# Moving VectorE's checks, maxima chain and statistics behind its own products, and two blocks of most chunks from VectorE to GpSimd, in a three-layer graph attention kernel

## The reference

```python
def gat_layer(x, src, dst, W, a_src, a_dst, b, n_nodes):
    h = x @ W
    s = h @ a_src
    d = h @ a_dst
    e = leaky_relu(s[src] + d[dst], 0.2)
    m = segment_max(e, dst)
    ex = exp(e - m[dst])
    z = segment_sum(ex, dst)
    alpha = ex / z[dst]
    return segment_sum(alpha[:, None] * h[src], dst) + b

h = relu(layernorm(x))
h = relu(gat_layer(h, ..., W1, a_src1, a_dst1, b1))      # layer 0: 128 -> 256
x = x + gat_layer(h, ..., W2, a_src2, a_dst2, b2)        # layer 1: 256 -> 128
h = relu(layernorm(x))
x = x + gat_layer(h, ..., W, att_src, att_dst, bias)     # layer 2: 128 -> 128, 1e-16 added to z
```

## Time and profile before

| | us |
|---|---|
| median of 3 runs | 685.88 (685.61 to 686.31) |
| the profiled execution's own time | 684.96 |
| its span (first to last record) | 683.1 |
| counting stage with chunk 0, until chunk 1's blocks | 205 |
| chunk 1, chunk 2 | 33.1, 36.4 |
| chunks 3, 4 and 5 | 38.3, 35.0, 36.1 |
| chunks 6, 7, 8 and 9 | 36.7, 32.3, 32.4, 34.7 |
| chunks 10 to 13 | 36.6, 29.7, 29.2, 29.2 |
| chunk 14 to the start of its last products, and the rest | 30.3, 8.1 |
| busy: PE, DVE | 591.5 (87%), 639.8 (94%) |
| busy: ACT, POOL | 484.3 (71%), 460.1 (67%) |

### The profile page before, as it was taken

How to read it: one execution, slowest core, us unless ns; L and a number is a source line. 1 busy time by engine, 2 the same in 40 slices (tenths; PEclk the granted TensorE clock), 3 DMA queues, 4 the chain that set the end, 5 groups by cost and what they waited for, 6 DMA issues and landing times.

```text
span 683.1 us, 13824 instructions
## 1 busy us (share of the span) xinstructions
PE 591.5 (87%) x5571; PEld 573.1 (84%) x5571; DVE 639.8 (94%) x911; ACT 484.3 (71%) x719; POOL 460.1 (67%) x448
## 2 busy tenths in 40 slices
PE   1729865899978999999999899999989989999994
PEld 1628755789878999899989799999988979999994
DVE  3999999999999989999987998999998899999993
ACT  0416544656969688887666788989886698888891
POOL 5579101889928565775954675858598678697883
PEclk9978986899999999999999999999999999999999
DMA  2410002000000000000100100000010010110001
GB/s 70 119 56 2 1 7 6 35 2 1 20 1 1 20 1 20 2 1 8 26 14 1 27 1 20 2 19 1 8 20 20 1 27 6 35 32 8 20 1 42
DMA packets 22325, 12.07 MB, mean 18 GB/s; under 512 B 12393, under 2 KB 20055, under 8 KB 22255
## 3 DMA queue, kind: packets, MB, share of 16 engines
q1 hardware_dynamic: 21455, 9.85, 6.3%
q0 software_dynamic: 800, 1.26, 0.6%
HBM read 9.47 MB, written 1.64 MB: 16 GB/s over the span
## 4 chain that ended last, share of the span: by engine, by line
DVE 51%; PE 29%; issue 8%; DMA 5%; POOL 4%; ACT 2%; POOLq 0%; DVEq 0%
PE ps L1813 21%; DVE scratch L951 20%; DVE ps L1067 15%; DVE scratch L1149 5%; DMA xr<-in_x 3%; POOL scratch L751 2%; DVE ps L1069 2%; DVE ps L1079 1%; PE ps L1866 1%; PE ps L1821 1%; PE ps L1844 1%; DVE scratch L1067 1%; DMA gathered<-in_edges,start_i 1%; DVE gathered L1149 1%; PE ps L1780 1%
## 5 line engine op out<-in xcount | busy, mean ns | idle before, releaser
L1813 PE MATMUL ps<-hB,scratch 125*125 125x129 f32 x3450 | 404.5, 276 | 21.1 <-DVE scratch L1149 17.6
L1813 PEld LDWEIGHTS ps<-hB,scratch 125*125 125x125 f32 x3450 | 390.9, 189 | 28.4 <-DVE scratch L1149 22.6
L751 POOL TENSOR_TENSOR scratch<-scratch,C 125x625 f32<-125x625 f32 x239 | 304.3, 1285 | 113.0 <-ACT scratch L1569 110.9
L1067 DVE SCALAR_TENSOR_TENSOR ps<-C,a_unit,ps 125x625 f32<-125x625 fp8e3 x330 | 275.4, 866 | 2.3
L1567 ACT ACTIVATE scratch<-gathered,r_neg 125x625 f32<-125x625 f32 x219 | 176.6, 806 | 20.3 <-PE ps L1813 19.2
L1569 ACT ACTIVATE scratch<-scratch,r_src 125x625 f32<-125x625 f32 x219 | 178.9, 817 | 7.1
L1452 ACT ACTIVATE C<-ps 125x1000 fp8e3<-125x1000 f32 x80 | 78.2, 1001 | 77.9 <-PE ps L1780 77.7
L1780 PE MATMUL ps<-scratch 128*128 128x125 bf16 x1250 | 93.4, 239 | 32.7 <-DVE scratch L951 30.7
L1780 PEld LDWEIGHTS ps<-scratch 128*128 128x128 bf16 x1250 | 85.7, 108 | 39.9 <-DVE scratch L951 37.8
L1149 DVE SCALAR_TENSOR_TENSOR scratch<-ps,r_src,C 125x625 f32<-125x625 f32 x121 | 104.1, 860 | 5.4 <-PE ps L1803 5.3
L951 DVE TENSOR_TENSOR scratch<-key_lo,ps 128x4096 bf16<-128x4096 bf16 (+3 forms) x41 | 89.3, 2178 | 0.0
(11 more groups left out here) (195 smaller groups left out, 444.6 us busy)
## 6 DMA issues: line engine op xcount, KB each, us to landing
gathered<-g_lines SPq DMA_DIRECT2D x15, 305.2 KB
xr<-in_x SPq DMA_DIRECT2D x1, 1562.5 KB
out<-xr SPq DMA_DIRECT2D x4, 312.5 KB
edge_sb<-in_edges SPq DMA_DIRECT2D x1, 805.7 KB
gathered<-ext_lines SPq DMA_DIRECT2D x5, 122.1 KB
w<-in_W SPq DMA_DIRECT2D x2, 128.0 KB
out<-xr SPq DMA_DIRECT2D x1, 187.5 KB
out<-xr SPq DMA_DIRECT2D x1, 125.0 KB
```

The costliest lines, as they stand in the source:

```text
L751: g.tensor_tensor(slot[s], slot[s], C5[:, q % NC, s, :], ALU.mult).then_inc(pool_done, 1)
L1067: v.scalar_tensor_tensor(dest, counts, unit[:, s:s + 1], top, ALU.min, ALU.max).then_inc(S.top_done, 1)
L1813: last = mm(ps[0:P, acc_at(t):acc_at(t) + HW], A[:, P * t:P * (t + 1)], feat, start=opens and t in (0, 3), stop=closes, skip_group_check=True)
```

## The change

It does three things.

**Later places.** MODE_AT puts the checks of chunks 6 and 11 at block 17 in place of block 2. In the tables for chunks 6 to 9 the chain goes from (2, 2, 3, 3) to (4, 4, 4, 5), kappa from 4 to 5, the sums' inverse from block 4 to 6, the statistics from 9 to 10. In chunk 1 the transposes go from block 14 to 16, and all that stands behind them by one or two blocks.

**Two blocks by POOL alone.** The table ALONE names blocks by layer: in layer 0 (chunks 2 to 4) 7, 9, 18 and 19, of which those are taken that ACT and POOL don't have already, which is two for each chunk (7 and 18 in chunks 2 and 4, 9 and 19 in chunk 3); in layers 1 and 2 blocks 8 and 20, for all chunks but the turns. These 22 blocks had been DVE's own products. POOL now makes each with a tensor_scalar and a product.

**What follows from it.** by_pool counts them among POOL's; first_maximum picks the buffer of row factors and the source factors by chunk and layer, and waits for the load at a chunk's first such block; ACT's loop leaves them out.

```diff
+        MODE_AT = 17
...
         FIRST_LAYER = (None,
-                       At(14, (15, 15, 16, 16), 16, (17, 17, 18), None, (23,), (21, 23, 27), (23, 25, 29), 25, 27),
+                       At(16, (17, 17, 18, 18), 18, (19, 19, 20), None, (24,), (23, 25, 29), (25, 27, 31), 27, 29),
...
         USUAL = (At(1, (3, 4, 5, 6), 6, (8, 9, 10), None, (14,), (12, 15, 21), (14, 17, 23), 18, 20),
-                 At(1, (2, 2, 3, 3), 4, (4, 4, 4), (9, 9), (11, 15), (15, None, 17), (14, 16, 19), None, None),
+                 At(1, (4, 4, 4, 5), 5, (6, 6, 6), (10, 10), (11, 15), (15, None, 17), (14, 16, 19), None, None),
...
         BEFORE_LAST = (At(1, (3, 4, 5, 6), 6, (8, 9, 10), None, (14,), (12, 14, 19), (13, 16, 21), 17, 18),
-                       At(1, (2, 2, 3, 3), 4, (4, 4, 4), (9, 9), (11, 15), (15, None, 17), (14, 16, 19), None, None))
+                       At(1, (4, 4, 4, 5), 5, (6, 6, 6), (10, 10), (11, 15), (15, None, 17), (14, 16, 19), None, None))
...
-        POOL_OF = tuple(pool_tiles(q) for q in range(Q))
+        ALONE = ((7, 9, 18, 19), (8, 20), (8, 20))
+
+        def alone(q):
+            return tuple(s for s in ALONE[q // NC] if s not in pool_tiles(q)) if q > 1 and not turn(q) else ()
+
+        POOL_OF = tuple(tuple(sorted(pool_tiles(q) + alone(q))) for q in range(Q))
...
         def by_pool(q, s):
-            return q == 0 and not (s % 4 == 3 and s < 16) or q == 1 and s < SECOND
+            return q == 0 and not (s % 4 == 3 and s < 16) or q == 1 and s < SECOND or s in alone(q)
...
-                if s == 0:
+                if s == min(p for p in POOL_OF[q] if by_pool(q, p)):
                     pool.wait_ge(ga_loaded, 16 * (q + 1))
...
-                g.tensor_scalar(slot[s], ga[q], LARGEST, r_src[0][:, s:s + 1], ALU.min, ALU.max).then_inc(first_max, 1)
+                g.tensor_scalar(slot[s], ga[q % 2], LARGEST, r_src[q // NC % 2][:, s:s + 1], ALU.min, ALU.max).then_inc(first_max, 1)
...
-                    if L and c == 1 and s == 2:
+                    if L and c == 1 and s == MODE_AT:
                         over_nodes(2 * L, ext_all, all_ready)
                         set_mode(L)
```

2 lines of the change are left out of this document (1 added, 1 removed).

## The result

The change makes the kernel slower: 694.59 us (693.76 to 695.49) against 685.75 us for the kernel before, a ratio of 1.0133 with a 95% interval of 1.0121 to 1.0146. That is +8.8 us where +5.5 was forecast; the time lies within the range (683.0 to 695.0), but only 0.4 us inside its upper end, and two of the four executions took more than 695. The profiled execution took 695.16 (span 692.4), 10.2 more than that of before.

The account below looks back on a forecast made before the run. TensorE and DVE were taken as nearly full, so only TensorE's pauses could give time. The chunk terms summed to +5.5 us, giving 690.5 for the profiled execution and 691.4 for the median, range 683.0 to 695.0.

Parts of the forecast that it names:

- What bounds the kernel: Whole kernel: TensorE and DVE are both nearly full, so time can only come out of TensorE's pauses.
- POOL's blocks: 22 blocks moved to POOL at 2.16 us each: 17.0 us off DVE, 47.5 onto POOL, in 11 chunks.
- Chunk 1 (+2.7): Chunk 1: later transposes make DVE wait at its reduction and TensorE wait for products 18, 20 and 22; +2.7 us.
- Chunk 3 (-0.5): Chunk 3: block 9 becomes POOL's, TensorE's wait moves to product 13, which comes 0.77 us sooner; -0.5 us.
- Chunk 6 (-3.0): Chunk 6: moving the checks removes the 3.60 us pause, then POOL and ACT decide; -3.0 us.
- Chunks 7 and 8 (+0.5): Chunks 7 and 8: later factor and POOL's block 15 replace pauses of 0.90 and 0.57; +0.25 us each.
- Chunk 9 (+3.6): Chunk 9: POOL ends the chunk later, 1.5 us from the later chain and 2.1 from block 20; +3.6 us.
- Layer 2: Chunks 11 to 14: -0.4 us in 11, +0.9 for 12 and 13 together, +1.7 in 14, block 20 making POOL late.
- (a): Rival, chance 0.16: DVE's relief reaches TensorE and its pauses at moved places go, 12.3 us, so 673.5; decided at chunk 7's block 15.
- (b): Rival, chance 0.15: POOL's added blocks hide, the rest as forecast, -1.0 us, so 684.9; decided at block 20 of chunk 9.
- (c): Rival, chance 0.12: chunk 1 costs nothing because something other than the reduction sets the pace; +2.8 us, 688.7.
- (d): Rival, chance 0.10: chunk 1's later pauses hold the low clock until block 20; +3.3 us, 694.7.

Follow-up runs that it names:

- block 2 and early transposes: Kernel before with checks split over chunks, layer 1's block 2 in chunks 6 to 9 by POOL alone, TensorE's transposes behind block 0: 679.83 against 685.83 us.

## Why the forecast was right, and what it missed

**What bounds the kernel.** Right. Time came only out of pauses of TensorE, and 12.4 us less work on VectorE (639.8 to 627.4 busy) bought nothing where something else stood behind the pause.

**POOL's blocks.** The price of 2.16 by the earlier trace rows held: 0.79 and 1.30 (516.74, 517.61 above). The statement of the Trainium skill, "GPSIMD Engine Reference", section "4.1 Engine selection", holds for block 20 in chunks 9, 11, 13 and 14, and the traces speak against it for block 8 of layer 2, which gained 0.4 a chunk in chunks 12 to 14 where POOL was waiting anyway.

**Chunk 1 (+2.7).** The mechanism was right to the rows: pause for product 15, transposes after 16, over 2 us of waiting at the reduction (2.44), about 1 us each for products 18 and 20 (0.94 and 0.60). The step that fell short is "I let the blocks take what they take there now". I took the low clock behind the gap as one number, and the end of the counting stage too. Where the first top is on time, the row costs 2.94 with the short stay at 0.50 (0.2 from the forecast) and 3.98 to 4.09 with the long one; in the first trace the stay was short and the first top 1.0 late. I also did not say that the hidden products move into chunk 2; that changes the split between the chunks and not the sum.

**Chunk 3 (-0.5).** The one wrong sign. That the wait would move from product 9 to product 13 was right, that the product would come 0.77 sooner was not. VectorE started it 20.70 us after the chunk's start, 20.53 before. The 0.77 was eaten by two delays: 0.65 by VectorE standing still while POOL worked on the products that its new block 9 had pushed back (last section), and 0.28 at a top in the chain, which the kernel without block 9 on POOL has too and whose cause no run shows. The pause grew to 1.9, and in one of the change's two traces the clock fell behind it: +0.17 or +1.84.

**Chunk 6 (-3.0).** Measured -3.12 in both traces, with the pauses for POOL's block 15 (0.91) and for ACT's normalising activations (0.44) that the forecast named. Checks and later chain without any block on POOL give the same -3.11, with 0.56 for ACT, so it is ACT's path that sets the -3.0, and POOL's block 15 adds nothing to it.

**Chunks 7 and 8 (+0.5).** +0.68. ACT waits 2.35 for the factor (430.95), and 0.88 and 0.46 take the place of 0.90 and 0.57. What the forecast did not see is that the checks cost chunk 7 a microsecond by themselves; "At block 17 the checks are free" is wrong, and block 20, taken off VectorE, hid 0.6 of it (+1.13 with checks and later chain, +0.49 with the change). That this sum came out to 0.2 is in part luck.

**Chunk 9 (+3.6).** +4.01 and +3.96. The factor came 1.6 later in the chunk (forecast 1.5), blocks 11 to 13 started 1.8 later, and from there to the last product POOL took 20.7 in place of 18.5, block 20's 2.2. TensorE's wait came at block 11 (3.94) and not at block 15, as the forecast had it; this pause and the low clock behind it cost nothing more, since POOL ended the chunk anyway.

**Layer 2.** -0.45, +1.01 and +1.71 for -0.4, +0.9 and +1.7. Chunk 14 is as forecast, but its wait came in two parts, 0.70 at block 20 and 1.38 at block 22, where the forecast has over 1.5 at block 22. In chunks 12 and 13 the sum is right and its parts are not: the forecast has a pause of 0.45 to 0.65 for block 20 in each, the trace has none in chunk 12 (+0.12) and 0.76 in chunk 13 (+0.89). By the runs of the parts, the moved checks cost chunk 12 1.10, which the forecast puts at nothing, and the two blocks taken off VectorE hide it (+0.12 together). This is luck.

**The sum.** Against the two traces 4.0 and 2.3 us are missing: chunk 1 (1.2), chunk 3 (2.3 or 0.7), chunk 9 (0.4) and chunks 7 and 8 (0.2), less 0.2 in chunk 10. The larger part is the low clock, which the forecast took from one trace: in the first trace that behind the pause of chunk 3 (1.7) and that in the last counting products, which made the first top 1.0 late; in the second the longer stay in chunk 1 (1.0).

**The rivals.** (a) fell at the point it named: POOL's block 15 was late in chunks 6 to 8. (b) fell at block 20 of chunk 9; its sum also took out too much, since 1.5 of the 3.6 is the chain's by the forecast's own words (1.50 measured), and with 2.1 in its place it would be +0.5, 686.4. And (c) fell by the run of chunk 1's row alone. (d) gave 694.7, next to the measured 694.59, but not for its reason: behind the waits for products 18 and 20 two blocks took 2.47 and three 3.76, with a granted clock of 1.00 from 230 to 237 us, so the low level did not hold until block 20.

## What to carry to other kernels

A busy share tells who is full, not who is waited for: before moving work off the busiest engine, list the waits of the engine that sets the pace and ask of each what stands right behind it. Work put on an engine with spare time is free only in the stretch where that engine is idle; block 8 of layer 2 gained 0.4 in each of three chunks and block 20, twelve blocks later on the same engine, cost up to 2.1 (chunk 14, +1.71 with it and -0.42 without). And work that nobody waits for (here the checks) belongs in a stretch where its engine has room: moving the checks of chunk 6 within a full stretch gained 3.6 us there and lost 0.95 in chunk 7, moving the larger part of them out kept all of it.

## What the runs showed of the hardware

**The price of a pause varies.** The same pause of 3.60 us in chunk 6 cost 15.05 us for the 120 records behind it in one kernel and 16.04 in another with the same instructions there, where 13.2 is full speed. Behind both the granted clock was 0.50, the level of 1.2 GHz, for differing times. Behind a pause of 2.94 (POOL's blocks alone, 13.53) it stayed at 1.00, and so it did behind one of 2.65 (checks and later chain, chunk 9), while behind one of 1.91 it fell (the change, chunk 3). Windows of TensorE in chunk 6 (stretch, length, busy, granted clock): two of the kernel with chunk 1's row alone, then one of the kernel before, behind the earlier trace rows's place, and one of the kernel with POOL's blocks alone:

```profile
401.00:402.00 1.00, 1.00 (x7) 0.50 0.00 0
402.00:403.00 1.00, 1.00 (x10) 0.87 0.00 0
...
397.00:398.00 1.00, 1.00 (x12) 1.00 0.00 0
...
396.00:397.00 1.00, 1.00 (x12) 1.00 0.00 0
```

The low level still held 5.0 us behind the start at 396.98, while before the change the blocks behind 393.20 were at full speed again 3.8 us on. A sum that takes one trace's slow blocks for granted is off by 1.0 (chunks 1 and 6) to 1.7 us (chunk 3) for such a pause.

**VectorE stops for POOL.** A step of 125 x 5 elements that takes 0.16 us took 0.81 in chunk 3 of the changed kernel and 0.78 in chunk 7 of the kernel with block 2 and early transposes. Each time it ended with POOL's product: 290.19 + 0.81 = 291.00 beside 288.40 + 2.58 = 290.98, and 422.99 + 0.78 = 423.77 beside 422.50 + 1.25 = 423.75. Without block 9 on POOL the step of chunk 3 took 0.16. The rows are the change's (two), those of the kernel with block 2 and early transposes (two), and the step without block 9:

```profile
290.19 0.81 DVE L1117 TENSOR_SCALAR held<-scratch 125x5 f32<-125x5 f32 x1
...
288.40 2.58 POOL L757 TENSOR_TENSOR scratch<-scratch,C 125x625 f32<-125x625 f32 x2
...
422.99 0.78 DVE L1119 TENSOR_TENSOR ps<-scratch,kappa 125x5 f32<-125x5 f32 x1
...
422.50 1.25 POOL L757 TENSOR_TENSOR scratch<-scratch,C 125x625 f32<-125x625 f32 x1 [0.31 <-ACT scratch L1576]
...
289.19 0.16 DVE L1117 TENSOR_SCALAR held<-scratch 125x5 f32<-125x5 f32 x1
```

The steps that were stopped read their operands from SBUF alone (held from the sums, and sums times kappa). The tops and own products, which read the other operand from PSUM, kept their 0.86 beside POOL. The Trainium skill, "SBUF — State Buffer", section "SBUF: two separate sides", says that VectorE and GpSimd share a pair of ports under an exclusive lock, taken by GpSimd's operations and by VectorE's in a two-port mode or with two SBUF inputs (the latter only against a GpSimd operation that reads SBUF), and that the loser waits for the other's whole instruction. The rows agree, to 0.02 us; in which mode the step with one input (held) ran, they don't show. Over the kernel the step of sums times kappa rose from a mean of 163 ns to 286 ns; it matters where an own product stands behind it.
